# Full-height first projections, a middle tile in four 64x64 tiles, variances summed by twos, and a new order of steps

## The reference

```
x = conv0(x); x = conv1(x)                       # conditional inverted bottlenecks
x = x + attention(LN(x)); x = x + ffn(LN(x))     # attention without softmax; FFN in quantised fp8
x = x + fourier(LN(x));   x = x + ffn(LN(x))
# conv: r = sigmoid(mean(x) Wr + br); weights mixed over 4 experts by r
#       h = relu(bn(x Wpw))      24 -> 96 channels   ("first projection")
#       h = relu(bn(dw3x3(h)))   depthwise, 96 channels
#       x = x + bn(h Wpwl)       96 -> 24            ("last projection")
# LN: (v - mean) / sqrt(var + eps) over the 24 channels of a position
```

## Time and profile before

| | |
|---|---|
| median of 3 runs | 2684.66 us (2683.72 to 2687.61) |
| the profiled execution | 2684.42 us |
| its span, first to last instruction | 2682.3 us |
| mean granted TensorE clock | 0.880 of 2.4 GHz |
| instructions | 49164 |

### The profile page before, as it was taken

One profiled execution on the slowest core, in us unless ns is written; L12 is line 12 of the kernel. 1 busy time (PEld: TensorE's weight loads), 2 busy tenths in 40 slices (PEclk: granted clock), 3 DMA queues, 4 the chain that ended last, 5 costly groups with the idle time before them and its releaser, 6 DMA issues.

```text
span 2682.3 us, 49164 instructions
## 1 busy us (share of the span) xinstructions
PE 2305.7 (86%) x19776; PEld 1278.3 (48%) x19776; DVE 1948.2 (73%) x3879; ACT 1678.5 (63%) x2824; POOL 69.0 (3%) x130
## 2 busy tenths in 40 slices
PE   3776988999889997999889998899879998987765
PEld 2233434664336733555336743465335553563552
DVE  4884977788857896697948788587866989466243
ACT  3344457756667567766856667766766668657654
POOL 1000000000000000000000000000000000000000
PEclk9887979989879897899879898899887998978766
DMA  4001001000020002000020000100010000000000
GB/s 132 1 1 19 1 1 19 2 2 1 1 36 2 1 1 37 2 1 1 1 37 2 1 1 2 36 2 1 1 28 2 2 1 1 20 1 1 19 1 19
DMA packets 108593, 29.56 MB, mean 11 GB/s; under 512 B 104144, under 2 KB 104272, under 8 KB 107984
## 3 DMA queue, kind: packets, MB, share of 16 engines
q1 hardware_dynamic: 108368, 26.41, 4.9%
HBM read 16.77 MB, written 9.63 MB: 10 GB/s over the span
## 4 chain that ended last, share of the span: by engine, by line
PE 59%; DVE 20%; ACT 12%; issue 4%; SPq 3%; DMA 1%; ACTq 0%; DVEq 0%
PE P L720 12%; PE P L701 9%; DVE acc L1417 7%; PE P L765 6%; PE P L915 4%; PE P L737 4%; PE P L741 3%; PE P L928 3%; SPq L574 2%; PE P L956 2%; PE P L756 2%; DVE SQ L1558 2%; PE P L866 2%; PE P L779 2%; PE P L940 1%
## 5 line engine op out<-in xcount | busy, mean ns | idle before, releaser
L1417 DVE SCALAR_TENSOR_TENSOR acc<-H,Dm,acc 128x784 f32<-128x784 f32 x1024 | 991.3, 1028 | 86.7 <-ACT acc L1083 86.3
L701 PE MATMUL P<-T,Wk 48*128 48x448 f32 (+5 forms) x768 | 402.5, 626 | 40.4 <-ACT H L1076 19.9
L720 PE MATMUL P<-H,diag 64*64 64x392 f32 x4608 | 401.0, 498 | 5.8 <-DVE T L1433 5.7
L1076 ACT ACTIVATE H<-P,biasA 128x448 f32<-128x448 f32 (+1 forms) x384 | 235.7, 621 | 216.2 <-PE P L701 145.9
L720 PEld LDWEIGHTS P<-H,diag 64*64 64x64 f32 x4608 | 171.5, 134 | 215.0 <-issue 201.9
L765 PE MATMUL P<-T,pack_b 112*112 112x448 f32 x448 | 245.0, 637 | 21.3 <-ACT mid L1124 6.6
L701 PEld LDWEIGHTS P<-T,Wk 64*128 64x128 f32 (+2 forms) x768 | 128.1, 205 | 177.5 <-ACT H L1076 73.8
L1106 ACT ACTIVATE acc<-P,biasT 128x392 f32<-128x392 f32 x128 | 69.1, 584 | 181.2 <-PE P L720 181.2
L1083 ACT ACTIVATE acc<-H,Dm 128x784 f32<-128x784 f32 x128 | 121.4, 949 | 49.5 <-PE P L741 47.2
L737 PE MATMUL P<-acc,Wk 64*112 64x392 f32 x256 | 118.7, 587 | 28.7 <-ACT acc L1112 28.6
L1433 DVE SCALAR_TENSOR_TENSOR T<-P,bias,T 112x392 f32<-112x392 f32 x128 | 78.6, 623 | 80.3 <-PE P L741 79.1
(11 more groups left out here) (192 smaller groups left out, 3800.7 us busy)
## 6 DMA issues: line engine op xcount, KB each, us to landing
xin<-in_x SPq DMA_DIRECT2D x224, 42.0 KB, 2.2
out_y<-arena SPq DMA_DIRECT2D x8, 1176.0 KB, 6.0
pack_b<-in_pack_b SPq DMA_DIRECT2D x1, 3820.5 KB, 17.4
arena<-in_pack_s SPq DMA_DIRECT2D x1, 1548.0 KB, 8.5
pack_a<-in_pack_a SPq DMA_DIRECT2D x1, 1084.0 KB, 5.3
pack_i<-in_pack_i SPq DMA_DIRECT2D x1, 320.0 KB, 3.1
arena<-in_pack_k SPq DMA_DIRECT2D x1, 192.0 KB, 3.2
```

What stands on the lines that cost most here:

```text
L701: pe.matmul(conv_rows(slice(0, 128), HB[(NP * s + e) % len(HB)], n), Wk1[rows, 128 * j:128 * (j + 1)], image_rows(T[q % 3][rows, :], a, n) ...
L720: last = pe.matmul(conv_rows(slice(64 * h, 64 * (h + 1)), CVB + r, HH), diag[64 * r:64 * (r + 1), tap, :], H1[64 * r:64 * (r + 1), slot(s, ...
L1076: act.activation(H1[:, slot(s, j), o:o + n, 1:1 + HW], conv_rows(slice(0, 128), HB[(NP * s + e) % len(HB)], n), ACT.Relu, bias=biasA[:, j, ...
L1417: ins = ve.scalar_tensor_tensor(a, H1[:, slot(s, j), r:r + SR, c:c + HW], Dm[:, j, tap:tap + 1], a, ALU.mult, ALU.add)
```

## The change

Four edits. `hidden` takes all 112 rows for every tile. `conv_out` does the middle tile in four matmuls of 64 rows by 64 or 48 columns, which lie in four different quarters of the array, and becomes two steps with the wait for `h2_ready` in the second. `layer_norm` on TensorE sums the variances of chunks 0 and 1 in one step behind the centring of chunk 2, of 2 and 3 behind chunk 4, of 4 and 5 behind chunk 6. TURNS has new lists for all four engines, with the same number of steps in each stream but two: on TensorE the d stream has 192 steps instead of 128, m 720 instead of 768 and b 1128 instead of 1176. The lists agree for the first 35 steps of TensorE, 75 of ScalarE, 28 of VectorE and 31 of GpSimd.

```diff
 TURNS = {
...
     "tensor": (
...
@@ hidden
-                        rows = {0: slice(0, 64), TJ: slice(0, R), 2: slice(64, R)}[j]
-                        pe.matmul(conv_rows(slice(0, 128), HB[(NP * s + e) % len(HB)], n), Wk1[rows, 128 * j:128 * (j + 1)],
-                                  image_rows(T[q % 3][rows, :], a, n), start=True, stop=True).then_inc(h1_psum.sem, 1)
+                        pe.matmul(conv_rows(slice(0, 128), HB[(NP * s + e) % len(HB)], n), Wk1[:, 128 * j:128 * (j + 1)],
+                                  image_rows(T[q % 3], a, n), start=True, stop=True).then_inc(h1_psum.sem, 1)
@@ conv_out
                 yield
                 pe.wait_ge(t2_ready.sem, t2_ready.at(q, 2 * (L * NS + s + 1)))
-                pe.wait_ge(h2_ready.sem, h2_ready.at(q, L * NV + 2 * (s + 1)))
-                for r in range(2):
+                for r, out_rows in enumerate((slice(0, 64), slice(64, R))):
                     for h in range(2):
                         rows = slice(64 * h, 64 * (h + 1))
                         w = Wk2p[rows, TJ * RC:TJ * RC + R] if r == h else Wk2t[rows, :]
-                        pe.matmul(conv_rows(slice(0, R), CVB + h, HH), w,
-                                  image_rows(acc[rows, (NT * s + TJ) % N2, :], HH * r, HH), start=(r == 0), stop=False)
+                        pe.matmul(conv_rows(out_rows, CVB + h, HH), w[:, out_rows],
+                                  image_rows(acc[rows, (NT * s + TJ) % N2, :], HH * r, HH), start=True, stop=False)
+                yield
+                pe.wait_ge(h2_ready.sem, h2_ready.at(q, L * NV + 2 * (s + 1)))
@@ layer_norm
-                    if c >= 1:
+                    if c >= 2 and c % 2 == 0:
                         yield
+                        variance(c - 2)
                         variance(c - 1)
```

More of the change, by code:

```diff
@@ L84 @@
     "gpsimd": (
-        "d7 b2 c11 m1 c10 m1 c5 b1 c4 b1 c3 m1 c3 b1 c4 b1 c2 m1 c4 b1 c4 b1 c2 m1 c4 b1 c4 b1 c2 m1 c4 b1 c4 "
-        "b1 c2 m1 c4 b1 c3 b1 c1 m1 b2 "
+        "d7 b2 c11 m1 c11 m1 c4 b1 c4 b1 c2 m1 c4 b1 c4 b1 c2 m1 c4 b1 c4 b1 c2 m1 c4 b1 c4 b1 c2 m1 c4 b1 c4 "
+        "b1 c2 m1 c4 b1 c4 b1 m1 b2 "
     ),
     "tensor": (
[44 rows of a table removed]
[46 rows of a table added]
     ),
     "scalar": (
[37 rows of a table removed]
[38 rows of a table added]
     ),
     "vector": (
[24 rows of a table removed]
[23 rows of a table added]
     ),
```

## The result

The changed kernel takes 2541.03 us (median of 4 runs, 2533.63 to 2543.59) against 2684.36 for the kernel before (4 runs). The ratio is 0.9459, with a 95% interval from 0.9436 to 0.9482. The profiled execution took 2543.51 us, with a span of 2541.4.

The account below looks back on a forecast made before the run. It took TensorE's own time as the bound: 57 + 62 - 4 = 115 us saved there, 83 us after shares on the chain, less 8, so 2684.7 - 75 = 2610 us, range 2558 to 2668.

Parts of the forecast that it names:

- What bounds the kernel: Whole span: TensorE's own time counts, busy 2305.7 of 2682.3 us, and 91% of the dense stretch.
- part 4: New order of steps on TensorE, ScalarE and VectorE: taken as neither gain nor loss, nothing credited.
- part 2: First projections on all 112 rows: 37 us from fewer shape changes, 11 within pieces, less 4 in the first quad.
- One in five at half clock: Middle tile of the last projection (L737): one record in five taken as run at half clock, giving 57 us.
- rival C: Granted clock: thinner TensorE work is granted less, giving back part of the gain; 2644 us, chance 0.08.
- Part 1: Middle tile of the last projection as four tiles in different array quarters: 57 us of TensorE time saved.
- Part 3: Layer norm variances of two chunks in one step: 4 us beyond the shape changes already counted.
- A: Whole kernel: all 115 us saved reach the end and the new order closes gaps; 2570 us, chance 0.17.
- B: VectorE, ScalarE and the input's DMA become the bound: only 31 us gained, 2654 us, chance 0.12.
- D: Middle tile: the four tiles don't stand abreast and save 0; 32 us remain, 2653 us, chance 0.03.
- E: New step's wait for L1106 stops TensorE's queue: slower, 2725 us at 1.8 us a strip, chance 0.07.
- F: First projections: full height takes overlap away in every quad; 15 us are left, 2670 us, chance 0.01.

Follow-up runs that it names:

- e11: The changed kernel with old shapes and split variance pairs, leaving only the new order and split step: 2642.08 us, ratio 0.9844 to the kernel before.
- e1: The kernel before, old order, with only the first projections put on all 112 rows: 2637.35 us, ratio 0.9799.
- e8: The kernel before, old order, each outer first-projection piece as two side-by-side matmuls of 112 rows by 64 columns: 2637.95 us, ratio 0.9823.
- e2: The kernel before, old order, with only the last projection's middle tile as four 64x64 tiles: 2657.54 us, ratio 0.9878.
- e6: The changed kernel with the middle tile back in 64x112 matmuls, in its own step: 2560.03 us, ratio 0.9528 to the kernel before.
- e7: The changed kernel with each variance pair split around a centring, same steps: 2566.73 us, ratio 0.9562 to the kernel before.
- e9: The changed kernel with the outer tiles' pieces back on 64 and 48 rows in the first quad only: 2537.14 us, ratio 0.9446 to the kernel before.
- e5: The changed kernel with the outer tiles' first projections back on 64 and 48 rows: 2595.12 us, ratio 0.9669 to the kernel before.

## Why the prediction was wrong

**What bounds the kernel** held in part: work taken from TensorE shortened the span. The two shapes in the old order gave 3.3% or 89 us, where my terms for them (57 and about 40 us of work, before the share that reaches the end) came to some 70. That the sum came even so near is luck, two errors against each other: the middle tile was put too high (47 us for 33), the full height too low (25 for 54).

**The step that failed first is part 4, "nothing" for the order.** With the split step it is worth 42 us (e11), more than half of the 68 us that the forecast missed. I compared the orders by which strip each step stands next to, found small shifts, and took small shifts for no effect. Of the two waits that I listed under the sum as not shrinking, the order shortened one, VectorE's ahead of its taps, by 39 us. Only the DMA's behaved as I said. Most of the order's gain is time at half clock (36 us in the ledger), a term that part 4 didn't have at all; its cause stays open.

**The second is part 2, the price of the full height.** I gave it 37 us of changes of shape (with the variances' share) and 11 within the pieces. The ledger has 19 us of work for it in e1, where 267 of the 399 changes of shape go; by my prices these and the pieces, less the first quad, would be 32. The first quad's loss was right: 4.0 us more for its first projections in e1, for the 4 that I took. The 0.09 us of a change of shape in the earlier trace rows is real, but e8 keeps most of the changes and is as fast as e1. What the rows gave, 54 to 56 us, came for the larger part through the clock.

**The clock was treated as a constant.** "One in five at half clock" multiplied the savings, and rival C let the clock move only down, by the argument that thinner work is granted less. I looked at nothing in the trace of before that could tell rows in use from busy time. By rival C's Trainium skill page ("TensorE: Matmul & The Clock Gate", section "HAM oscillation — how this bites in real kernels") idle gaps bring the half rate back. Here TensorE's idle time grew by 12 us, its idle stretches of 2 us and more went from 33 (135 us) to 41 (159 us), and still the time at half clock fell (mean granted clock 0.880 to 0.907). So fewer or shorter gaps are not what raised it.

**Part 1** was right in its mechanism and its size of work: 43 us in the ledger of e2 and 40 between after and e6, at full clock, where I had 48 (64 x 0.75). The share that reached the end was 33 us in the old order (0.58 of the 57, not 0.83) and 19 in the new, where VectorE holds 40% of the chain. For this block the share on the chain of waits was too high an estimate. **Part 3** had the pairs' work as some 22 us in all and 16 in the ledger; 28 us at the end; e7's interval reaches some 8 us to either side and the changed kernel's 6. So the small term of 4 us was mis-sized too.

**Rivals.** A was nearest (2570), for the reason of the order, but it lacked the clock. B's sign shows in the chain, which now runs through VectorE, without the loss. C went the other way. D is ruled out by the 0.81 us block. E asked for 1.2 us of waits a strip; TensorE now waits 7.2 us in all for L1109 at the middle tile, 0.1 a strip, seen in this group of after:

```profile
L737 PE MATMUL P<-acc,Wk 64*64 64x392 f32 x128 | 56.7, 524 | 7.4 <-ACT acc L1109 7.2
```

F is ruled out: the full height gained 54 us in the old order and 56 in the new. What the first quad lost by it e9 puts at 4 us, within its interval.

## What to carry to other kernels

Don't price an order of steps by how far it moves them: shifts of a strip at most were worth 42 us here. Where an order can't be timed on paper, leave room in the range on both sides. A matmul whose contraction fills half of the array may be worth widening to all rows, with zero weights in the added ones, even where no time of its own is saved, if no other matmul could run beside it and the profile shows the clock at half rate in part of the span. And a share on the chain of waits is a weak estimate of what a shorter step returns: the middle tile gave 33 and 19 us where the share said 47, the pairs 28 us for 16 us of work.

## What was not expected of the hardware

With the same columns streamed and zeros in the added rows' weights, 112 rows in place of 64 and 48 raised the mean granted clock from 0.880 to 0.893 and more in the old order, and from 0.889 to 0.907 in the new (e5 to after); 65 rows for 64 in one of the two tiles left it at 0.880, where 96 and 112 rows with the same step lengths ran at 0.885 to 0.894. The order of steps with the split step raised it as well, to between 0.884 and 0.892, with the same rows. Runs of one kernel show what it is worth: the seven runs of the kernel before beside e1 went from 2678.04 us at 0.884 to 2693.95 us at 0.877.
